# Project stage of a decoder kernel: convolved rows turned ahead of the SiLU, normalisation on ScalarE, gate terms inside the last block, the delta stage's first loads issued there

## What is computed

```python
normed = (x - mu) * rsqrt(var + EPS) * ln_w + ln_b
q = causal_conv_silu(normed @ Wq, conv_q)      # four taps along time, then SiLU
k = causal_conv_silu(normed @ Wk, conv_k)
v = causal_conv_silu(normed @ Wv, conv_v)
beta = sigmoid(normed @ Wb)
g = -exp(A_log) * softplus(normed @ Wa + dt_bias)
q = l2norm(q) * HK ** -0.5 ; k = l2norm(k)     # per head of 64
# a recurrence over time in chunks follows, then normed @ Wg as the output's gate
```

## Time and profile before

| what | value |
|---|---|
| median of 3 runs | 1940.9 us (1935.88 to 1942.78) |
| the profiled execution's own time | 1944.99 us, span 1943.2 us |
| busy share of the span: TensorE | 81% |
| VectorE | 59% |
| ScalarE | 41% |
| GpSimd | 30% |
| project stage, within the span | 0 to about 315 us |
| delta stage starts | 316.2 us |

### The profile page before, as it was taken

The page is one execution under the profiler, slowest core; times in us unless marked ns, Lnnn a source line. Parts: engine busy times, 40 slices in busy tenths (PEclk is TensorE's granted clock), DMA queues, the critical chain, the costliest instruction groups (busy, mean ns, idle before and its releaser), DMA issues. The chain is left out here.

```text
span 1943.2 us, 31223 instructions
## 1 busy us (share of the span) xinstructions
PE 1581.9 (81%) x10722; PEld 1115.9 (57%) x10722; DVE 1145.9 (59%) x2425; ACT 803.9 (41%) x1715; POOL 589.1 (30%) x515
## 2 busy tenths in 40 slices
PE   5898972378889889967589999999747999999980
PEld 3444441377777777743247776667634666666650
DVE  4998993456666566433235677777753554555545
ACT  3777771023333333433345555555312333333324
POOL 0322234312223221011023355554542333333330
PEclk9898985679999888988799999999868999999995
DMA  2232326644544443203611221310421111111117
GB/s 83 87 140 86 140 86 161 157 100 122 124 130 121 121 121 88 70 26 118 218 51 50 89 73 59 117 34 23 137 92 31 44 48 47 45 47 47 44 39 262
DMA packets 189895, 178.73 MB, mean 92 GB/s; under 512 B 88391, under 2 KB 148475, under 8 KB 189627
## 3 DMA queue, kind: packets, MB, share of 16 engines
q1 hardware_dynamic: 175131, 149.75, 25.6%
q0 software_dynamic: 10400, 22.95, 3.6%
q10 hardware_dynamic: 4224, 4.19, 0.6%
HBM read 116.73 MB, written 60.11 MB: 91 GB/s over the span
## 5 line engine op out<-in xcount | busy, mean ns | idle before, releaser
L533 DVE SCALAR_TENSOR_TENSOR conv_y<-conv_in,taps,conv_y 128x512 f32<-128x512 f32 x192 | 165.3, 876 | 19.3 <-ACT conv_y L401 14.7
L2236 POOL DMA_INDIRECT y<-o,idx x71 | 83.4, 1175 | 241.8 <-DVE o L2379 234.1
L2315 ACT ACTIVATE xsT<-pX 128x256 f32<-128x256 f32 x71 | 27.3, 384 | 303.8 <-PE pX L2260 303.8
L1679 PE MATMUL xQ<-late,last 128*128 128x512 f32 x256 | 125.2, 612 | 16.5 <-ACT late L1835 7.8
L2271 PE MATMUL pG<-w_gu,xsT 128*128 x284 | 135.5, 600 | 1.2 <-ACT xsT L2315 1.1
L2292 PE MATMUL pD<-late,hT 128*128 x568 | 134.2, 379 | 0.0
L2271 PE MATMUL pU<-w_gu,xsT 128*128 x284 | 133.8, 593 | 0.0
L322 PE MATMUL ps_j<-xnT,w_qkv 128*128 128x512 f32 x256 | 131.3, 650 | 0.0
L1645 POOL TENSOR_TENSOR sc<-sc,den 128x1232 f32<-128x1232 f32 x32 | 72.0, 2249 | 174.6 <-DVE den L2061 174.5
L2292 PEld LDWEIGHTS pD<-late,hT 128*128 128x128 f32 x568 | 102.5, 190 | 11.0
L2375 DVE TENSOR_TENSOR o<-pD,late 128x256 f32<-128x256 f32 x71 | 30.1, 425 | 120.7 <-PE pD L2292 120.7
(11 more groups left out here) (317 smaller groups left out, 3773.1 us busy)
## 6 DMA issues: line engine op xcount, KB each, us to landing
qkvg<-tok SPq DMA_DIRECT2D x8, 2048.0 KB, 6.7
qkvg<-gate SPq DMA_DIRECT2D x8, 1024.0 KB, 8.8
step<-step SPq DMA_DIRECT2D x32, 256.0 KB, 4.2
qk<-qkvg SPq DMA_DIRECT2D x32, 256.0 KB, 4.5
vb<-qkvg SPq DMA_DIRECT2D x32, 256.0 KB, 4.6
gt<-qkvg SPq DMA_DIRECT2D x32, 256.0 KB, 2.8
y<-y SPq DMA_DIRECT2D x16, 512.0 KB, 8.2
xin<-in_x SPq DMA_DIRECT2D x11, 512.0 KB, 3.9
```

Of the source, the lines that this page charges most:

```text
L533: y = nc.vector.scalar_tensor_tensor(conv_y[m % 4][:], conv_in[b][:, m, k:k + BT], taps[:, m, k:k + 1], conv_y[m % 4][:], ALU.mult, ALU.add)
L1679: mm = pe.matmul(Q[:], w_q[:, c, j * P:(j + 1) * P], x1T[:, c, :], start=c == 0, stop=c == KD - 1)
L2236: nc.gpsimd.indirect_dma_start(out=s["y"].rearrange("t p d -> (t p) d"), out_offset=bass.IndirectOffsetOnAxis(ap=idx[j % 8][:, 0:1], axis= ...
```

## The change

Five things, all in the project stage and at the entry of the delta stage:

- The tiles are turned right after the convolution: TensorE waits for `conv_done` and turns `conv_y`; `act_y` and ScalarE's pass L384 are gone, and the copy of `ps_t` into `tok` takes the SiLU.
- The normalisation is done by ScalarE as Identity with scale and bias by row; VectorE makes the bias, `shift = -mean * rstd`. `block_sd` moves to j == NCT, the normalisation stands at j == NCT + 2, ahead of the head norm's root.
- The loops of all engines run over three pairs of blocks, and the fourth pair is written out, so that the work for blocks that don't exist is left out, and the gate terms can stand between the channel tiles of the last block. The tables are stored before the last `tok`.
- The first loads are ordered anew, and the engines wait for parts of them.
- The first `load_scores` of the delta stage are issued by SyncE at the end of the project stage; its buffers and semaphores are allocated outside. GpSimd's memsets stand behind the four diagonals, and the waits on them and on the weights move to their first users.

```diff
@@ project stage, SyncE @@
+            sp.dma_start(con[:], a["consts"]).then_inc(con_in, 16)
+            for k, w in enumerate((a["L0_attn_ln_w"], a["L0_attn_ln_b"])):
+                sp.dma_start(ln_wb[:, k, :], w.rearrange("(k p) -> p k", p=P), allow_slow_non_contiguous=True
+                             ).then_inc(ln_in, 16)
...
+                    if n is LAST:
+                        sp.wait_ge(gate_taken, n * BLK + BLK)
+                        sp.dma_start(tok_v[n][:, :, QKV:QKV + DV], gate[b][:]).then_inc(tok_out[b], 16)
+                        sp.wait_ge(aT_done, 1)
+                        sp.dma_start(s["step"], aT[:]).then_inc(tok_out[0], 16)
+                        sp.wait_ge(cT_done, 1)
+                        sp.dma_start(s["cum"], cT[:]).then_inc(tok_out[0], 16)
+                        sp.wait_ge(gb_done, 1)
+                        sp.dma_start(s["gb"].rearrange("t p c -> p t c"), gb[:]).then_inc(tok_out[0], 16)
 
                     sp.wait_ge(scaled, n + 1)
...
             sp.wait_ge(tok_out[0], 32 * (BLOCKS // 2) + 48)
+            first_scores(sp, s)
             sp.wait_ge(tok_out[1], 32 * (BLOCKS // 2))
@@ TensorE @@
-                        pe.wait_ge(silu_done[m % 2], n * (NCT // 2) + m // 2 + 1)
+                        pe.wait_ge(conv_done, n * NCT + m + 1)
...
-                                              act_y[m % 2][:, t * P:(t + 1) * P], con[:, C_ID:C_ID + P])
+                                              conv_y[m % 4][:, t * P:(t + 1) * P], con[:, C_ID:C_ID + P])
...
+                        if n is LAST and j == NCT + 1:
+                            gate_sums()
@@ ScalarE @@
+            def normalise(n, b):
+                if const(n) and n > LAST:
+                    return
+                act.wait_ge(shift_done, n + 1)
+                for t in range(BLK):
+                    xn = nc.scalar.activation(xin[b][:, t, :], xin[b][:, t, :], ACT.Identity, bias=shift[:, t:t + 1],
+                                              scale=rstd[:, t:t + 1])
+                xn.then_inc(xn_done, 1)
...
-                                             ACT.Copy).then_inc(tok_taken[m % 2], 1)
+                                             ACT.Silu).then_inc(tok_taken[m % 2], 1)
...
-                            act.wait_ge(silu_done[j % 2], n * (NCT // 2) + max(j // 2 - 1, 0))
+                            act.wait_ge(tokT_done[j % 2], n * (NCT // 2) + max(j // 2 - 1, 0))
...
-                        if 2 <= j < NCT + 2:
-                            silu(j - 2)
...
+                        if n is LAST and j == 3:
+                            gate_exponentials()
+                        if j == NCT:
                             block_sd(n + 2)
+                        if j == NCT + 2:
+                            normalise(n + 2, b)
                             act.wait_ge(ss_done, n + 1)
                             nc.scalar.activation(rn[:], ss[:], ACT.Sqrt, bias=eps[:, 1:2]).then_inc(norm_sd, 1)
@@ VectorE @@
-                for t in range(BLK):
-                    xn = nc.vector.tensor_scalar(xin[b][:, t, :], xin[b][:, t, :], mv[:, t, 0:1],
-                                                 rstd[:, t:t + 1], ALU.subtract, ALU.mult)
-                xn.then_inc(xn_done, 1)
+                nc.vector.scalar_tensor_tensor(shift[:], mv[:, :, 0], -1.0, rstd[:], ALU.mult, ALU.mult
+                                               ).then_inc(shift_done, 1)
...
+                        if n is LAST:
+                            if m == 0:
+                                gates_begin()
+                            if m == 3:
+                                gates_ratio()
+                            if m == 4:
+                                gates_series((13, 11, 9))
+                            if m == 5:
+                                gates_series((7, 5, 3))
+                            if m == 6:
+                                gates_decay()
+
+                    norm_terms(n + 2)
                     dve.wait_ge(sq_done, n * 2 + 2)
...
-                    normalise(n + 2, b)
                     logits_out(n + 1)
-            gates_out()
...
+            pairs(dve, blocks)
+            gates_end()
+
+
+def first_scores(sp, s):
+
+    tables, rows, steps, keys, landed = s["first"]
+    for b in range(BATCH):
+        load_scores(sp, s, b * CHUNKS, tables[b], rows[b], steps[b], keys[b], landed[b])
@@ delta stage, GpSimd @@
             for b in G:
                 diagonal(0, b)
+            nc.gpsimd.memset(eps[:], EPS).then_inc(set_up, 1)
+            for t in (U_all, T_all):
+                nc.gpsimd.memset(t[:], 0.0).then_inc(set_up, 1)
+            for b in G:
+                nc.gpsimd.memset(S[b][:], 0.0).then_inc(set_up, 1)
+                for k in R:
+                    nc.gpsimd.memset(UF[k][b][:], 0.0).then_inc(set_up, 1)
+            for b in G:
                 key_ends(0, b, 0)
```

More of the change, by code:

```diff
@@ L199, in view_heads, with pairs @@
             return t[:, :, lo:lo + n * d].rearrange("p t (h d) -> p t h d", d=d)
+        LAST = BLOCKS - 1
+        const = lambda n: isinstance(n, int)
+        def pairs(eng, body):
+            with eng.Fori(0, BLOCKS // 2 - 1) as i:
+                body(i)
+            body(BLOCKS // 2 - 1)
         @block.sync
@@ L519, in _, with blocks @@
                 moments(b, b, 0)
-                normalise(b, b)
+                norm_terms(b)
             logits_out(0)
-            with dve.Fori(0, BLOCKS // 2) as i:
+            def blocks(i):
                 for b in range(2):
@@ L549, in _, with load_scores @@
                                             ).then_inc(norm_r, 1)
-                    normalise(n + 2, b)
                     logits_out(n + 1)
-            gates_out()
+            pairs(dve, blocks)
[4 more added lines that the diff above has]
+        load_scores(sp, s, b * CHUNKS, tables[b], rows[b], steps[b], keys[b], landed[b])
+def load_scores(sp, s, tile, table, rows, step, keys, landed):
+    sp.dma_start(table[:], s["gb"][tile]).then_inc(landed, 16)
+    for k in range(2):
+        sp.dma_start(rows[HP * k:HP * k + HP], s["cum"].rearrange("(n t r) j -> n r t j", t=2, r=2)[tile, k].unsqueeze(0)
+                     .broadcast_to([HP, 2, P])).then_inc(landed, 16)
+    sp.dma_start(step[:], s["step"].rearrange("(n k) j -> n k j", k=H)[tile].unsqueeze(0).broadcast_to([P, H, P])
+                 ).then_inc(landed, 16)
+    sp.dma_start(keys[:], s["qkvg"][tile, :, 0:2 * DK]).then_inc(landed, 16)
 def delta_stage(nc, a, s):
@@ L569, in delta_stage @@
         eps = sb("eps2", [P, 1])
-        gbt = per("gbt", [P, GATES])
-        step = per("step", [P, H, P])
-        qk = per("qk", [P, 2 * DK])
-        grow = per("grow", [P, 2, P])
+        gbt, grow, step, qk, qk_in = s["first"]
         E = per("E", [P, H, P])
@@ L2499, in build @@
         s["tile_r"] = sb("tile_r", [P, FT], I32)
-        project_stage(nc, a, s)
-        delta_stage(nc, a, s)
+        with ExitStack() as first:
+            each = lambda n, shape: [first.enter_context(nc.sbuf_tensor(f"{n}{b}", shape, F32)) for b in range(BATCH)]
+            s["first"] = (each("gbt", [P, GATES]), each("grow", [P, 2, P]), each("step", [P, H, P]),
+                          each("qk", [P, 2 * DK]), [sem(f"qk_in{b}") for b in range(BATCH)])
+            project_stage(nc, a, s)
+            delta_stage(nc, a, s)
         context_stage(nc, a, s)
```

168 lines of the change are left out of this document (84 added, 84 removed).

## The result

| | before | after |
|---|---|---|
| median of 5 runs | 1940.9 us (1935.88 to 1945.1) | 1926.81 us (1922.57 to 1927.16) |
| the profiled execution's own time | 1944.99 us | 1926.99 us, span 1924.9 us |

The ratio is 0.9924, with a 95% interval of 0.9903 to 0.9946: the change takes 10.5 to 18.8 us off, 14.1 by the medians. A second set of runs of the changed kernel on another chip gave 0.9921 (0.9903 to 0.9938). The forecast was 1925.9.

The account below looks back on a forecast made before the run. VectorE's convolution tap passes were taken as the bound, with block boundaries mattering most. Terms -7.2 - 6 + 3.4 - 10.7 + 5.5 = -15.0 took the median from 1940.9 to 1925.9 us; own range 1918 to 1937, 8 in 10 1915 to 1940.

Parts of the forecast that it names:

- Start: Project stage start: logits product at 15.0 us instead of 22.2, waiting for the last weights alone; gain 7.2 (6.5 to 8).
- Blocks 1 to 6: Six middle blocks, T (start of a block's sum of squares) to T: -6 us (-7.7 to +1), mostly from removed waits.
- The SiLU: Inside blocks: ScalarE loses 8 passes of 0.64 per block; gives only part of the 7.6 us waits and a shorter way from T.
- The normalisation: Block boundary: moving four passes to ScalarE frees nothing; six boundaries cost -0.07 each, or +0.25 if ScalarE is a little late.
- The chain of the forecast: Block boundary, from T: shift, four passes, table load, root, reciprocal, scaling sum to 8.34; convolution starts about T + 8.4.
- Last block: T of block 6 to T of block 7: 35.2 us against 31.8, +3.4, as gate terms lie exposed on VectorE.
- Tail: After block 7's T: table of gates issued at T + 8.8, gain 11.7, less 1 for the shared queue: -10.7.
- rival C: Tail gives less: table lands 4 late behind the shared queue, key-end pairs still cost 1.62; 1932.2 us, chance 0.17.
- Delta entry: Delta stage start: early loads delay the barrier; block diagonals out 32.2 after the table lands against 26.5, +5.5 (3 to 9).
- A: Block boundary: scaling does not hold the convolution, which starts at T + 7.1, saving 1.3 at six boundaries; 1918.1 us, chance 0.15.
- B: Blocks: ScalarE sets the pace; if table switches hold it twice their row, 23 us over six boundaries; 1951.5 us, chance 0.08.
- The signs: Signs: logits near 15, convolution T + 8.3 to 8.8, table under T + 10; wrong if a block stays over 32.5 us.

Follow-up runs that it names:

- the six traces: Profiles with ScalarE's normalisation in looped blocks: after twice, gate terms moved back, first loads moved back, diagonals first, late start; five distances take 158.60 to 159.79 us.

## Why the prediction was right, and what in it was wrong

- **Start.** Forecast 15.0 for the logits product, measured 14.65 (-7.6). x had landed by 4.8, as the sum needed. The first T moved by 8.9; the 1.3 more lie inside block 0, where the kernel with the SiLU alone also starts its first T 2.1 early. The forecast gave block 0 nothing for that.
- **Blocks 1 to 6.** Forecast -6, measured -6.4 (-5.5 to -7.2 over the six traces), out of terms that were each off. The SiLU gives -9.8, where at most the 7.6 of rows 2 was allowed, of which 1.1 lies before the first T: that it also takes ScalarE's lateness off the boundary, 0.40 each, is written in rows 3 (the table load 1.24 after T) and was not read, and neither was it that these waits come with a low clock. The normalisation costs 3.9 to 5.7 over five blocks, where -0.07 each was put. The chain of the forecast was right: 8.34 from the end of the last convolution, measured 8.20 without loops (the held pass ends at 152.96, less its own 0.75, from 144.01). But it was compared with the 8.47 of before, which the other part of the change had already shortened to 8.07, and it holds only where ScalarE is on time. That ScalarE has no slack was said; that it starts late, and is made late again by loads at the loop's head and by a late TensorE, was not, and its price (0.25 each) was taken too small. And block 6 has lost its own moments as well, which the forecast gave to block 7 only: its distance is 29.12, against 31.36 with the SiLU alone. A part of these 2.2 is the clock's (0.83 behind T against 0.67); with VectorE's normalisation and like clocks the moments are worth 0.7 (30.62 against 31.36) to 1.4 (29.33 against 30.7). In the profiled pair -9.8 + 5.6 - 2.2 = -6.4.
- **Last block.** Forecast 35.2, measured 34.97.
- **Tail.** The table went out at T + 8.6 (forecast 8.8), and landed 9.3 later, no later than before (9.9), with the token store right behind it in the same queue. The 1 us for the shared queue was not lost, nor the 4 of rival C.
- **Delta entry.** Diagonals out at landing + 32.6 (forecast 32.2, which is 5.7 over the 26.5 before; the sum took 5.5), 19.3 after the stage's start (forecast 19.0). Its parts partly cancel: the four diagonals of GpSimd took 5.9 (forecast 5.0), the pairs of key ends 0.7 each (forecast 0.8).
- **Rivals.** A: the convolution does start before the scaling's end, as A has it, but its first pass is held to that end, so nothing is gained. That the scaling is what holds it is read from the rows; no run changed the scaling alone. B: the engine named was the right one, the price wrong; no drain. C: not seen.
- **The signs.** Most came out: logits product, table of gates, stage start, diagonals. Two did not. The convolution was to start 8.3 to 8.8 after T and starts 6.7 to 9.3 after it. And a block over 32.5 us was named as a sign of being wrong: one of the blocks of after is, 32.85, for the clock's lateness and the loop's loads together; in its second trace none is.
- **The sum.** In the profiled executions the steps sum to -18.5 against -15.0 forecast. By the medians the gain is 14.1, within an interval of 10.5 to 18.8. The median of 1926.81 lies 0.9 from the forecast. Much of that nearness is luck: within the blocks two terms missed by about 4 and 4 to 6 us in opposite directions, and start and tail did 3.5 us better than forecast, which shows in the traces (18.5 apart) and not in the medians (14.1). The bounds that the forecast gives with its terms add up to 1920 to 1940, not to its 1918 to 1937; the median lies inside both.

## What to carry to other kernels

When a change has several parts on one critical place, make the sum of each against the kernel with the other parts in it, not against the kernel before: here a pass taken off ScalarE made the boundary shorter, and work put on ScalarE then cost more than the old boundary showed. Moving work off the busiest engine gains nothing where it stood beside other work anyway, and on the receiving engine what counts is not its busy share (ScalarE: 129 of 160 us) but whether it stands between two steps of the chain. A mean clock over a stage can hide that its low stretches fall on the same place of a loop: compare the distances of single blocks with the clock just before, and take a second trace of the same kernel before explaining a difference of one or two us. At the entry of a stage, read the order of the queue's program too: a transfer whose data are ready can wait 9 us behind two others that nobody needs yet.

## What the runs showed of the hardware

- A table load takes 1.28 us and the next activation starts 0.01 to 0.02 behind it, also with three loads in 4.3 us (220.37 to 224.65).
- At the head of each turn of this loop the program loads ScalarE's table again, at the first activation and at the first of another function behind it, though the right one is loaded (150.79 and 154.35, against none when the pairs are written out).
- A VectorE tap pass that starts while GpSimd multiplies `tok` in place ends 0.5 us behind it: 1.83 us instead of 0.75.
- TensorE's granted clock falls to its lower level (0.50, which is 1.2 GHz) at most block boundaries, where TensorE waits for the last tiles (2.3 us ahead of 112.72 in after). The mean over the eight us behind T is 0.58 to 1.00, and the same boundary of the same kernel can show 0.61 in one execution and 0.79 in the next; the eight projections there took 6.18 and 4.79 us.
- One DMA issue took 8.35 us on ScalarE's queue while a 2 MB store and other loads were under way.
